# Cross attention 2: one bank of scores in 28 goes through VectorE and GpSimd instead of ScalarE

## The reference

```
q, k, v = heads of  x @ Wq.T,  ctx @ Wk.T,  ctx @ Wv.T     # 16 heads, 8 wide
weights = sigmoid(q k^T / sqrt(8))                         # 1024 x 6404 per head
x = x + concat(weights @ v) @ Wo.T
```

## Time and profile before

| | us |
|---|---|
| timed runs, median (lowest, highest) | 5762.28 (5759.06, 5765.22) |
| profiled execution, its own time | 5761.91 |
| its span | 5760.2 |
| TensorE busy in the span | 5149.8 |
| ScalarE busy | 3459.5 |
| VectorE busy | 3193.3 |
| GpSimd busy | 2226.9 |
| ScalarE busy in this stage's sigmoids (L3471) | 726.2 |
| VectorE idle before its copies in this stage (L3480) | 726.4 |

### The profile page before, as it was taken

The page is one execution under the profiler, slowest core; times in us unless marked ns, Lnnn a source line. Parts: engine busy times, 40 slices in busy tenths (PEclk is TensorE's granted clock), DMA queues, the critical chain, the costliest instruction groups (busy, mean ns, idle before and its releaser), DMA issues. The chain is left out here.

```text
span 5760.2 us, 67076 instructions
## 1 busy us (share of the span) xinstructions
PE 5149.8 (89%) x26368; PEld 1640.3 (28%) x26382; DVE 3193.3 (55%) x3561; ACT 3459.5 (60%) x3536; POOL 2226.9 (39%) x1118
## 2 busy tenths in 40 slices
PE   8879999999999999789897699998886788888889
PEld 3323333333333333233343311111432111111123
DVE  5687777777777772225622300000257998888723
ACT  4466666666666666511122499998125677777861
POOL 1139899998989999716442000000000000000000
PEclk8889999999999999999998899999896899999999
DMA  1000000000000000000000300000204000000011
GB/s 51 15 1 1 4 1 5 1 5 1 4 5 1 5 1 5 21 22 1 2 0 10 112 20 20 13 9 5 79 25 136 2 11 12 12 17 7 6 46 31
DMA packets 67590, 104.45 MB, mean 18 GB/s; under 512 B 12100, under 2 KB 52134, under 8 KB 65164
## 3 DMA queue, kind: packets, MB, share of 16 engines
q1 hardware_dynamic: 67070, 99.34, 5.3%
q10 hardware_dynamic: 206, 0.83, 0.0%
HBM read 74.58 MB, written 25.43 MB: 17 GB/s over the span
## 5 line engine op out<-in xcount | busy, mean ns | idle before, releaser
L2509 ACT ACTIVATE Pr<-ps,key_bias 128x1024 f32<-128x1024 f32 x816 | 865.3, 1111 | 658.9 <-PE ps L2384 658.8
L2611 DVE TENSOR_REDUCE red<-ps 128x2 f32<-128x1024 f32 (+1 forms) x767 | 904.8, 1181 | 423.2 <-PE ps L2371 422.4
L2707 POOL TENSOR_TENSOR Ps<-Ps,Pr 128x1024 f32<-128x1024 f32 x400 | 946.7, 2367 | 144.8 <-ACT Pr L2509 144.0
L2716 POOL TENSOR_TENSOR Ps<-Ps,Pr 128x1024 f32<-128x1024 f32 x400 | 945.5, 2364 | 0.0
L3341 DVE TENSOR_REDUCE red<-ps 128x1 f32<-128x512 f32 (+3 forms) x1024 | 877.8, 908 | 94.6 <-PE ps L3214 75.2
L3297 ACT ACTIVATE Pr<-ps 128x1024 f32<-128x1024 f32 x816 | 786.3, 1021 | 229.3 <-PE ps L3224 228.6
L2384 PE MATMUL ps<-Q,Kr 64*128 64x512 f32 x3264 | 805.5, 610 | 43.7 <-DVE ps L2344 24.9
L2404 PE MATMUL ps<-Pr,Vc 128*64 128x512 f32 x3264 | 790.1, 605 | 0.0
L3471 ACT ACTIVATE Pr<-ps 128x2048 f32<-128x2048 f32 x467 | 726.2, 2024 | 1.6 <-PE ps L3434 1.6
L2344 DVE CAST ps<-seeds 128x1024 f32<-128x1024 bf16 x499 | 601.3, 1222 | 187.6 <-ACT Pr L2509 172.5
L3214 PE MATMUL ps<-Kp,Q 52*128 52x512 bf16 (+1 forms) x1664 | 442.1, 412 | 170.8 <-DVE red L3341 125.4
(11 more groups left out here) (577 smaller groups left out, 5050.6 us busy)
## 6 DMA issues: line engine op xcount, KB each, us to landing
L_dram_K<-parts SPq DMA_DIRECT2D x26, 384.0 KB, 3.0
Kp<-L_dram_K SPq DMA_DIRECT2D x14, 624.0 KB
L_dram_K<-parts SPq DMA_DIRECT2D x26, 256.0 KB, 2.9
wB<-L_ffn_shares SPq DMA_DIRECT2D x1, 6144.0 KB
w<-L_ffn_experts_w_dram SPq DMA_DIRECT2D x24, 256.0 KB
Kp<-L_dram_K SPq DMA_DIRECT2D x14, 416.0 KB
over<-cross_dram_inverse SPq DMA_DIRECT2D x14, 256.0 KB
wB<-L_ffn_shares SPq DMA_DIRECT2D x1, 3584.0 KB, 12.8
```

The lines of the kernel that those rows point to most:

```text
L2509: nc.scalar.activation(Pr[:, t % 4, half].rearrange("p a n -> p (a n)"), ps[:, 2 * half:2 * half + 2, :].rearrange("p a n -> p (a n)"), AC ...
L2611: nc.vector.tensor_reduce(red[:, i // C % 2, q, :, i % C], ps[:, b:b + 2, 0:ctx.keys_in(i % C)], AX, ALU.max).then_inc(*reduced.up())
L2707: nc.gpsimd.tensor_tensor(into, into, src, ALU.add).then_inc(*summed0.up())
L2716: nc.gpsimd.tensor_tensor(into, into, src, ALU.add).then_inc(*summed1.up())
```

## The change

The banks i = 6, 34, 62, ... (every 28th) whose key tile is from 3 to KT - 2 - 5 = 44 are no longer part of ScalarE's sigmoid; the unit's ScalarE instruction has two banks in place of three. VectorE copies the bank from PSUM to `raw` (two buffers). GpSimd computes the sigmoid as (1 + (1/e)^x)^-1: a power with a tile of 1/e, an addition of 1, a power with a tile of -1, into `Pw` (two buffers). TensorE multiplies it with v five key tiles later, ahead of that step's own four products. TensorE's scores of unit u also wait until the copies from unit u - 2 are done, since they overwrite the bank.

```diff
+    LATER = 5
+    by_pool = [i for i in range(6, 4 * T, 28) if 3 <= i // 4 % KT <= KT - 2 - LATER]
+    raw, Pw = k.tile(stack, "raw", [128, 2, HALF]), k.tile(stack, "Pw", [128, 2, HALF])
+    per_e, minus = k.tile(stack, "per_e", [128, HALF]), k.tile(stack, "minus", [128, HALF])
...
         def scores(u):
             if u >= 2:
                 nc.tensor.wait_ge(*sigmoid_done.at(u - 1))
+                for n, i in enumerate(by_pool):
+                    if unit_of(i) == u - 2:
+                        nc.tensor.wait_ge(*brought.at(n + 1))
...
             nc.tensor.wait_ge(*sigmoid_done.at(unit_of(4 * t + 3) + 1))
+            for n, i in enumerate(by_pool):
+                if i // 4 == t - LATER:
+                    half, a = i // 2 % 2, i % 2
+                    at = 32 * (2 * half + a)
+                    nc.tensor.wait_ge(*pool_done.at(n + 1))
+                    nc.tensor.matmul(ps[at:at + 8, 7, :], lhsT=A.V[:, kt - LATER, 2 * p + a, :], rhs=Pw[:, n % 2, :], start=False, stop=True, skip_group_check=True)
             for i in range(4 * t, 4 * t + 4):
-                half, a = i // 2 % 2, i % 2
-                at = 32 * (2 * half + a)
-                mm = nc.tensor.matmul(ps[at:at + 8, 7, :], lhsT=A.V[:, kt, 2 * p + a, :], rhs=Pr[:, i % 21, :], start=False, stop=True, skip_group_check=True)
+                if i not in by_pool:
+                    half, a = i // 2 % 2, i % 2
+                    at = 32 * (2 * half + a)
+                    mm = nc.tensor.matmul(ps[at:at + 8, 7, :], lhsT=A.V[:, kt, 2 * p + a, :], rhs=Pr[:, i % 21, :], start=False, stop=True, skip_group_check=True)
...
         for u in range(U):
             n = min(first(u + 1), 4 * T) - first(u)
+            if first(u) + n - 1 in by_pool:
+                n -= 1
...
         for p in range(P):
+            for n, i in enumerate(by_pool):
+                if i // 4 // KT == p:
+                    nc.vector.wait_ge(*scored.at(unit_of(i) + 1))
+                    if n >= 2:
+                        nc.vector.wait_ge(*pool_done.at(n - 1))
+                    nc.vector.tensor_copy(raw[:, n % 2, :], ps[:, i % 7, :]).then_inc(*brought.up())
             nc.vector.wait_ge(*weighed.at(KT * (p + 1)))
...
+    def pool():
+        nc.gpsimd.memset(per_e[:], math.exp(-1.0)).then_inc(*constants_set.up())
+        nc.gpsimd.memset(minus[:], -1.0).then_inc(*constants_set.up())
+        nc.gpsimd.wait_ge(*constants_set.at(2))
+        for n, i in enumerate(by_pool):
+            nc.gpsimd.wait_ge(*brought.at(n + 1))
+            nc.gpsimd.tensor_tensor(raw[:, n % 2, :], per_e[:], raw[:, n % 2, :], ALU.pow).then_inc(*pool_step.up())
+            nc.gpsimd.wait_ge(*pool_step.at(2 * n + 1))
+            nc.gpsimd.tensor_scalar(raw[:, n % 2, :], raw[:, n % 2, :], 1.0, None, ALU.add).then_inc(*pool_step.up())
+            nc.gpsimd.wait_ge(*pool_step.at(2 * n + 2))
+            if n >= 2:
+                nc.gpsimd.wait_ge(*weighed.at(by_pool[n - 2] // 4 + LATER + 1))
+            nc.gpsimd.tensor_tensor(Pw[:, n % 2, :], raw[:, n % 2, :], minus[:], ALU.pow).then_inc(*pool_done.up())
```

More of the change, by code:

```diff
@@ L3384, in small_sigmoid @@
     U = unit_of(4 * T - 1) + 1
-    scored, sigmoid_done, weighed, out_copied, out_stored0, out_stored1, zeroed = k(
-        "scored", "sigmoid_done", "weighed", "out_copied", "out_stored0", "out_stored1", "zeroed")
+    scored, sigmoid_done, weighed, out_copied, out_stored0, out_stored1, zeroed, constants_set, brought, pool_step, pool_done = k(
+        "scored", "sigmoid_done", "weighed", "out_copied", "out_stored0", "out_stored1", "zeroed", "constants_set", "brought", "pool_step", "pool_done")
     out_stored = (out_stored0, out_stored1)
     Pr = k.tile(stack, "Pr", [128, 21, HALF])
+    LATER = 5
+    by_pool = [i for i in range(6, 4 * T, 28) if 3 <= i // 4 % KT <= KT - 2 - LATER]
+    raw, Pw = k.tile(stack, "raw", [128, 2, HALF]), k.tile(stack, "Pw", [128, 2, HALF])
+    per_e, minus = k.tile(stack, "per_e", [128, HALF]), k.tile(stack, "minus", [128, HALF])
     Oc = k.tile(stack, "Oc", [128, 2, HALF])
@@ L3488, in small_sigmoid @@
     dve()
+    pool()
     k.barrier(A.first_in0, A.first_in1, *A.key_in, *out_stored, *out.landed())
```

## The result

| | before | changed |
|---|---|---|
| median of the timed runs, us | 5760.67 | 13150.65 |
| ratio, 95% interval | | 2.2834 (2.2805 to 2.2862) |
| span of the profiled execution, us | 5760.2 | 13148.4 |

The account below looks back on a forecast made before the run. ScalarE's sigmoids were taken to bound cross attention 2's sigmoid stage, TensorE following closely. The 0.41 us saved became a 0.57 us delay, 48 times 27 us, on 5761.9: about 5789 us, range 5748 to 5830.

Parts of the forecast that it names:

- Step 3: GpSimd's added two powers and one addition per bank: about 9 us (3.2 to 10.7), hidden within the 12 us allowed.
- Rival 2: GpSimd's chain becomes the bound if a power exceeds 5.1 us: 5839 us at 6 us, 6031 at 8; 20 in 100.
- the signs that I named for it: TensorE released by GpSimd's Pw, and periods above 13 us.
- Step 1: ScalarE's sigmoid drops from three banks to two: 0.41 us saved a bank, 20 us if nothing stood in the way.
- Step 2: 48 VectorE copies from PSUM, 0.69 us each, on an otherwise idle engine: cost nothing.
- Step 4: TensorE's late product makes four records queue in one column group: 0.90 us more per tile, bounds 0 and 0.90.
- The 6 us of room for a first call: First GpSimd call to a freshly loaded kernel could make the first bank late, once: sum at most 6 us higher.
- Where the two meet: Long product tile behind the shortened sigmoid's scores: next four-bank sigmoid starts 0.57 us later, 48 times, 27 us.
- rival 1: Late product costs TensorE little: at no cost -0.23 us a bank, 5751 us; at half price 5768; 25 in 100.
- Rival 3: Two-bank sigmoid's pitch is like three banks', so no saving: still 5789 us; counted within the forecast's 55 in 100.

Follow-up runs that it names:

- Experiment 2: Changed kernel with multiplications for both GpSimd powers and the 48 late products left out: 5739.96 us, ratio 0.9961 to the kernel before.
- experiment 8: Multiplications for the powers, no late products, plus four full GpSimd power chains on constants for which nobody waits: 5737.66 us, ratio 0.9966 to the kernel before.
- experiment 1: Changed kernel with both GpSimd powers replaced by multiplications, all else the same: 5766.52 us, ratio 1.0012 to the kernel before.
- 3: Changed kernel with multiplications for the powers and the late product seven key tiles on in place of five: 5744.95 us, ratio 0.9972 to the kernel before.
- 4: Changed kernel with multiplications for the powers and the late product behind scores that have no products behind them: 5739.80 us, ratio 0.9964 to the kernel before.
- experiment 6: Changed kernel with the second power a multiplication and the first taking five forms in turn (columns, partitions, constants or scores): 5938.81 us in one execution.
- experiments 5: Changed kernel with the second power a multiplication and the first over 64 of 512 columns: 5826.66 us, ratio 1.0115 to the kernel before.

## Why the prediction was wrong

**Step 3, GpSimd's price, is the step that failed.** I bounded a power by 4.36 us, the longest GpSimd instruction of the trace (a memset of 5120 columns), and took 9 us for the chain. It is 165.9 us. No row of before held a power, and the rows that I took for an upper end were of other operations: they bounded nothing. The estimate beside the Trainium skill's rule (GPSIMD Engine Reference, 3.1 Elementwise side by side, about 3 operations a cycle) went the same way: it asked what a power of 5 us could hold and not what a power needs. At that page's 1.2 GHz the measured 160 ns a column are 192 cycles, by the rule an estimate of some 570 operations. No run here shows how many operations a power has.

**Rival 2 was the right mechanism**, with 20 chances in 100, and its formula holds far outside the range I gave it: 48 x (165.9 - 12.3) = 7373 us, measured 7390. Of the signs that I named for it all came: TensorE released by `Pw`, periods above 13 us, everything queued behind the late product. Its price list ended at powers of 8 us, and the range at 5830 us took in only its cheap third. An operation that no row prices should have held the top of the range open.

**Step 1** took 0.41 us a bank for the saving on ScalarE. Experiment 2's 20.2 us for 48 banks looks like just that, but part of it is luck: inside a pair the period fell by 0.33 us, as the release by unit 0's sigmoid held the rest back, and periods at the ends of pairs got shorter too.

**Step 2** was right: the copy is 0.69 us, and besides GpSimd, which needs its result, nobody waited for it.

**Step 4** was near: 0.84 us for the late product in place of 0.90, and the full-width scores do wait for the long group.

The 6 us of room for a first call (step 3) did not show: in experiment 8 the first power starts 0.08 us after the memset before it ends, and is as long as the others.

```profile
3282.35 0.53 POOL L3499 MEMSET minus<- 128x512 f32 x1
3282.96 82.17 POOL L3502 TENSOR_TENSOR Pw<-per_e,minus 128x512 f32<-128x512 f32 x1
```

**"Where the two meet"** had the right place and sign and twice the size or more: 0.30 us a period where I had 0.57, and 6.3 us in all where I had 27. It erred twice. I started the long tile where that tile starts in the earlier trace rows, behind scores that four-bank records of 2.1 to 2.2 us had released. Their length is not fixed: right after a wait a four-bank record is 1.88 us, and in the gapless stream before it rose as far as 2.41. With a wait in each period it stays short, and TensorE is released earlier. For the same reason rival 1's floor of -0.23 us was too high (-0.33 measured). And I multiplied by 48 where the two meet in 40 periods. Rival 1, "the late product costs little", is false at this place (experiments 1 against 2) and true at two others (3 and 4).

**Rival 3** is false: in experiment 2 the two-bank sigmoid has a pitch of 1.00 us even while it is held back, and not 1.33.

## What to carry to other kernels

Before an operation moves to an engine on which the trace has never seen it, price that operation by itself: rows of other operations are no upper bound, and one kernel like that of experiment 6 settles it. An engine that sits idle is not a cheap engine: 166 us of GpSimd stood against 0.42 us of ScalarE. Where a consumer waits in order, the chain's length against the period decides all, and a product put off should go where the array has a hole or a vacant column group, since the same product cost 0.55 us at one place and nothing at another.

## What the runs showed of the hardware that I had not expected

- GpSimd's power: 0.160 us a column in fp32, the same for 16 and for 128 partitions, for constants and for scores (experiments 5 and 6); an addition of a scalar 1.50 us and a product 1.27 us for 512 columns.
- Eight powers of 82 us beside the stage changed nothing that could be measured on the other engines (experiment 8).
- An activation's record is longer the longer ScalarE has run without a gap: for four banks 1.88 us after a wait and 1.93 us six units later (experiment 1), 2238 ns on average in the gapless stage before, at the same pitch of 1.75 us. The pitch is what ScalarE pays; the record's end is what a consumer waits for (in experiment 2 the scores start 0.05 us after it).
- TensorE's granted clock was 0.50 in 140 us without work. Its first scores after that took 1.04 us, those at 6161.33 again 0.60 us.
- A tensor_scalar over SBUF on VectorE took 427 ns where tensor_tensor and scalar_tensor_tensor took 692, and a reciprocal 3353 (all 128x512, fp32).
